# Causal attention: VectorE's split of a half's maxima placed directly behind the last of them

## The reference

```python
h = _layernorm(x, ln_w, ln_b)                        # then a causal depthwise convolution of 3 taps along T
q, k, v = jnp.split(h @ attn_w, 3, axis=-1)          # 16 heads of 8
q = q * cos + _rotate_half(q) * sin                  # k likewise
scores = jnp.einsum('bqhd,bkhd->bhqk', q, k) / jnp.sqrt(jnp.float32(D))
scores = jnp.where(causal, scores, jnp.float32(-1e+30))
p = jax.nn.softmax(scores, axis=-1)
y = jnp.einsum('bhqk,bkhd->bqhd', p, v).reshape(B, T, C)
x = x + y @ proj_w
```

## Time and profile before

| | us |
|---|---|
| median of 3 runs | 1636.36 (1632.52 to 1644.97) |
| profiled execution: its own time, its span | 1630.4, 1628.7 |
| causal attention in it | about 234 (236 to 470) |

### The profile page before, as it was taken

The page is one execution under the profiler, slowest core; times in us unless marked ns, Lnnn a source line. Parts: engine busy times, 40 slices in busy tenths (PEclk is TensorE's granted clock), DMA queues, the critical chain, the costliest instruction groups (busy, mean ns, idle before and its releaser), DMA issues. The chain is left out here.

```text
span 1628.7 us, 23696 instructions
## 1 busy us (share of the span) xinstructions
PE 1406.0 (86%) x9145; PEld 715.1 (44%) x9145; DVE 987.6 (61%) x1770; ACT 687.7 (42%) x1204; POOL 628.2 (39%) x626
## 2 busy tenths in 40 slices
PE   7868786988989999899868999899999877889984
PEld 3345443433334444444334444454445433355542
DVE  4898939777742211468566773745556344588866
ACT  2444432766742000257534774244434432355522
POOL 2487734354223221333124312533421312356762
PEclk8889997989999999879987998999999978999996
DMA  5000010000020000100001002000000010000000
GB/s 111 0 1 0 1 48 1 1 1 1 1 82 1 1 0 0 53 1 1 11 0 54 2 2 47 1 2 1 2 1 2 2 31 1 7 1 2 2 1 28
DMA packets 17382, 20.65 MB, mean 13 GB/s; under 512 B 7835, under 2 KB 13195, under 8 KB 16760
## 3 DMA queue, kind: packets, MB, share of 16 engines
q1 hardware_dynamic: 15440, 17.33, 3.6%
q10 hardware_dynamic: 1832, 1.80, 0.5%
HBM read 17.94 MB, written 1.05 MB: 12 GB/s over the span
## 5 line engine op out<-in xcount | busy, mean ns | idle before, releaser
L1852 DVE CUSTOM_DVE_ANT_0 P<-P,L2f_mask 128x128 f32<-128x128 f32 (+3 forms) x256 | 118.5, 521 | 99.9 <-PE P L1744 99.9
L1029 DVE TENSOR_REDUCE L0f_nm<-P 128x2 f32<-128x768 f32 (+3 forms) x88 | 97.5, 1120 | 38.1 <-PE P L926 37.9
L2028 PE MATMUL P<-L0m_hm,L0m_w 128*128 128x512 f32 x256 | 112.2, 597 | 0.0
L1822 ACT ACTIVATE L2f_prob<-P 128x1024 f32<-128x1024 f32 x80 | 80.6, 1025 | 73.1 <-PE P L1756 73.1
L1663 POOL TENSOR_SCALAR_AFFINE_SELECT L2f_prob<-L2f_prob 128x512 f32<-128x512 f32 x64 | 39.9, 638 | 161.4 <-ACT L2f_prob L1822 161.4
L983 ACT ACTIVATE L0f_prob<-P 128x512 f32<-128x512 f32 x160 | 86.9, 610 | 33.8 <-PE P L937 32.5
L1744 PE MATMUL P<-L2f_ks,L2f_qs 48*128 48x512 f32 (+3 forms) x512 | 90.9, 467 | 0.3 <-DVE L2f_nm L1852 0.3
L1756 PE MATMUL P<-L2f_qs,L2f_ks 49*128 49x256 f32 (+3 forms) x512 | 84.5, 444 | 3.1 <-DVE L2f_nm L1852 2.3
L2431 POOL TENSOR_TENSOR L3x_exm<-L3x_exm,L3x_rec 128x2048 f32<-128x2048 f32 x16 | 72.4, 4530 | 24.1 <-DVE L3x_rec L2617 24.1
L1306 PE MATMUL P<-ident,L0x_pv 128*128 128x128 f32 x384 | 53.7, 305 | 27.1 <-POOL L0x_pv L1207 27.1
L880 POOL TENSOR_SCALAR_AFFINE_SELECT L0f_prob<-L0f_prob 128x512 f32<-128x512 f32 x64 | 39.9, 638 | 95.2 <-ACT L0f_prob L983 88.3
(11 more groups left out here) (578 smaller groups left out, 3329.5 us busy)
## 6 DMA issues: line engine op xcount, KB each, us to landing
L0m_w<-in_L0m_w SPq DMA_DIRECT2D x1, 2048.0 KB, 8.0
L0f_va<-in_L0f_va SPq DMA_DIRECT2D x3, 512.0 KB, 5.3
L0x_prod<-in_x SPq DMA_DIRECT2D x2, 512.0 KB, 5.9
L0x_segi<-in_segb SPq DMA_DIRECT2D x1, 1024.0 KB, 18.2
L0m_w<-in_L0m_w SPq DMA_DIRECT2D x1, 1024.0 KB, 10.0
out<-out_o SPq DMA_DIRECT2D x4, 256.0 KB, 2.4
L1x_va<-in_va SPq DMA_DIRECT2D x3, 256.0 KB, 3.1
L1x_vr<-in_vr SPq DMA_DIRECT2D x3, 256.0 KB, 4.1
```

What stands on the lines that cost most here:

```text
L1029: nc.vector.tensor_reduce(S.nm[:, qt, first:first + 2 * many].rearrange("p (i e) -> p e i", e=2), P[:, bank:bank + 2, 0:many * width].rear ...
L1822: nc.scalar.activation(S.prob_of(b, g)[:, at:at + 2, :], P[:, bank:bank + 2, :], ACT.Exp).then_inc(*S.act_done.up())
L1852: m = nc.vector.tensor_tensor_reduce(out=at, in0=at, in1=mask[:, T - width:T], scale=1.0, scalar=-3.0e38, op0=ALU.add, op1=ALU.max, accum_ ...
L2028: m = mm(P[:, slot(b, i) + part, :], w1[:, e, part * 512 + i * 128:part * 512 + i * 128 + 128], hm[b % 2][:, e, :], start=e == 0, stop=e = ...
```

## The change

Two edits in causal_order, none to the instructions themselves.

```diff
-STEP_causal_order = """sa0 R0 w0 w1 R1 la A0 B0 t0 k0 ... R8 p0 A5 mb x0 R9 B1 sa1 mc p1 sb1 B5 mt B7 x1 R10 conv C1 out C3 sc1 max res""".split()
+STEP_causal_order = """sa0 R0 R1 la w0 w1 A0 B0 t0 k0 ... R8 p0 A5 mb x0 R9 B1 sa1 mc p1 R10 sb1 B5 max mt B7 x1 conv C1 out C3 sc1 res""".split()
...
-    lead = [(k, 0, n) for n in (2, 3) for k in ("t1", "tk")] + [(k, 1, n) for n in range(QT) for k in "px"] + [("conv", 2, 0)]
-    order += spread_between(lead, rounds(0)) + [("max", 0, 0)]
+    lead = [(k, 0, n) for n in (2, 3) for k in ("t1", "tk")] + [(k, 1, n) for n in range(QT) for k in "px"]
+    order += spread_between(lead, rounds(0)) + [("max", 0, 0), ("conv", 2, 0)]
```

More of the change, by code:

```diff
@@ L793, in split_pair @@
         ops.tensor_copy(k[:, :, :, 1], k[:, :, :, 4]).then_inc(*self.qk_ready.up())
-STEP_causal_order = """sa0 R0 w0 w1 R1 la A0 B0 t0 k0 R2 B2 A1 lb A2 R5 A4 C0 k1 R4 A6 lc lt rec sb0 sc0 B6 R3 B4 A3 R7 A7 ma C2 B3 R6 t1 turn R8 p0 A5 mb x0 R9 B1 sa1 mc p1 sb1 B5 mt B7 x1 R10 conv C1 out C3 sc1 max res""".split()
+STEP_causal_order = """sa0 R0 R1 la w0 w1 A0 B0 t0 k0 R2 B2 A1 lb A2 R5 A4 C0 k1 R4 A6 lc lt rec sb0 sc0 B6 R3 B4 A3 R7 A7 ma C2 B3 R6 t1 turn R8 p0 A5 mb x0 R9 B1 sa1 mc p1 R10 sb1 B5 max mt B7 x1 conv C1 out C3 sc1 res""".split()
 def causal_order(STEP=STEP_causal_order):
```

## The result

The changed kernel takes 1668.05 us (1665.09 to 1670.35), 1.0184 of the kernel before, with a 95% interval of 1.0141 to 1.0227; timed again on another chip (f_both below) it is 1.0200, 1.0157 to 1.0244. It is slower by about 31 us. The forecast was 13 us more, and its range ended at 1659: the sign was right, the size was not.

What follows compares the result with a forecast made beforehand. It took PE, busy for 86% of the span, as the bound. Terms -1.2 + 4.4 - 1.2 + 5.6 + 0.4 + 1.2 + 4.2 = +13.4 us gave 1649 us from a median of 1636.4, range 1636 to 1659.

Steps and rivals of the forecast that it cites:

- The split no longer ends last: At the ends of halves, w0's wait for the split, 20.8 us in all, would be gone or under 1 us.
- p + 3.75: Half 0 before: split's end counted from p, when p1 is done and PE takes up B5; forecast p + 3.4.
- rival 4: The split is hardly earlier where R10 follows p1, 0.4 us; counted within the forecast, with no chance of its own.
- C1 waits for x1, four times 4.3: Halves 0 to 3: x1 behind R10 and the split starts C1 4.0 us later, PE idle for 4.3.
- Rival 3: x1 does not stop PE at C1, so shifts and drops there are gone: -9 us, 1627; chance 0.13.
- The pair decides behind halves 1 and 3, and the shift goes through behind 0 and 2: POOL's pair sets t0 behind halves 1 (-1.2) and 3 (+0.4); w1's shift passes through behind 0 (+4.4) and 2 (+5.6).
- A0's exponential then follows w0 about 0.4 closer: Halves 4 to 6, with la ahead of w0: A0 follows w0 about 0.4 us closer, offsetting part of the delay.
- at most +0.9 each, nothing at least: Halves 4 to 6, which have no p1: delay from la behind tv, ahead of w0; +1.2 us taken for the three.
- Drops at the ends of all four halves ... 2 x 2.1 = +4.2: PE's clock falls behind the C1 waits of halves 0 to 3; costs 2.1 us each behind 0 and 2 only.
- Rival 2: The low clock stays 6.5 us or more behind each C1 stall: +20.6 us, 1657; chance 0.17.
- Rival 1: The clock is not dropped where it costs, or comes back at once: +9 us, 1645; chance 0.20.
- -1.2, between 0 and -2.3: The lead: convolution behind the split lets split and w0 go earlier, a gain of 1.2 us, at most 2.3.

Runs made afterwards that it cites:

- f_both: The changed kernel itself, timed again on another chip: 1.0200 of the kernel before.
- e6_x1_first: The changed kernel with x1 alone put back ahead of R10 and the split: 1653.67 us, 1.0098 of the kernel before.
- f_stall: The changed kernel with la put back behind w1, so x1 stays behind R10 and the split: 1.0093 of the kernel before.
- f_neither: The kernel before with only the convolutions behind the split and R1 ahead of w0: 0.9995 of the kernel before.
- the cells: Four kernels, x1 ahead of or behind the split and la behind or ahead, R1 ahead and convolutions behind: 0.9995 to 1.0200 side by side on one chip.
- e7_r1_only: The kernel before with the convolutions behind the split and R1, without la, ahead of w0 and w1: 1629.49 us, 0.9965.
- f_la: The kernel before with the convolutions behind the split and R1 and la ahead of w0, x1 in its old place: 1.0041.
- e2: The kernel before with the convolutions behind the split and R1 and la ahead of w0 and w1: 1649.45 us, 1.0120.
- e1: The kernel before with only the convolutions moved behind the split: 1632.86 us, 0.9989.
- e4_busy: The changed kernel with 16 matmuls of no use to the result in front of C1 in halves 0 to 3: 1665.62 us, 1.0183.
- e9_la_late: The kernel before with convolutions behind the split, R1 ahead of w0, and la ahead of w0 in halves 4 to 7 alone: 1636.13 us, 1.0019.
- e12: The changed kernel with la put back behind w1 in half 7 alone: 1653.40 us, 1.0115 of the kernel before.
- e8_lead_busy: The kernel before with convolutions behind the split and matmuls of no use to the result on PE in the lead: 1636.63 us, 0.9999.

## Why the prediction was right in sign and wrong in size

**The split no longer ends last: right.** Its wait fell from 20.8 us to 2.9. In half 0 that is not because the split came early: it ends 3.8 us behind R10's first product (301.69 to 305.47), where 3.4 was forecast and before it was p + 3.75, as rival 4 has it. It is w0 that comes later.

**C1 waits for x1, four times 4.3: right.** Four times 4.1, and e6_x1_first shows the cause: x1 ahead of R10 takes the wait away, and 14 us with it. The size of the wait was worked out from rows of before and met to 5%. Rival 3 (x1 does not stop PE) is refuted.

**The pair decides behind halves 1 and 3, and the shift goes through behind 0 and 2: right but for 1.2 us.** -1.2 forecast and measured behind half 1; +0.4 forecast and +1.6 measured behind half 3; +7.7 against +8.3 behind half 2, clock included. f_stall has this part alone: +14.9 in the trace of the stage, of which 4.1 stand in lead and half 0 of f_neither too.

**"A0's exponential then follows w0 about 0.4 closer" and "at most +0.9 each, nothing at least", for R1 and la ahead of w0: this step failed.** I priced la as a shift of w0 by its length and noted only in passing that it had covered ACT's copies. The forecast had about 3 us for la (1.0 each behind halves 0 and 2, and the +1.2; the working beside "+0.9" gives 1.0); the cells give it 1.0% of the kernel, some 16 us. The same edit for R1 costs nothing that can be told (e7_r1_only). What is seen in the traces is the cover lost: nine waits for ACT's copies, 5.0 us in all, against none or 0.3 with la behind. With x1 ahead of the split they use up what the shorter wait for the split gives (5.0 us in f_la). The stage is longer by 5 or 6 us with la ahead, in about equal parts of idleness and of slower matmuls (f_la less f_neither 2.5 and 3.2, e2 less e1 2.6 each); with x1 behind the split it is longer by 11 or 12, of which 6 or 7 are idleness and 5 slower matmuls. In half 7 the low clock came with la ahead, and for the clock there the forecast had no term at all.

**"Drops at the ends of all four halves ... 2 x 2.1 = +4.2": right where it looked.** The drops behind the C1 waits came. At the end of half 0 the changed kernel is at +9.5 and +9.1, e4_busy, at a clock of 1.00, at +4.4; less the 2.0 to 2.7 of the lead, the drop cost 2 to 3 us for 2.1 forecast. Rival 1 (the clock is not dropped where it costs) is refuted by these 2 to 3 us as far as one trace of each kernel can do it; the prediction's remark that the second rival is the case of no loss should name the first. Rival 2 (the low clock stays) has part of its condition: in this trace the clock is at 0.50 for 7 us behind C1, past its 6.5, but back at 1.00 when t0 starts at 315.38. It does not have its places: behind halves 1 and 3 the pair still hides the low clock. What the term lacked is the drops away from the C1 waits, in half 7 and in the lead.

**The lead, "-1.2, between 0 and -2.3": not found.** Lead and end of half 0 without the C1 wait are +3.6 in e1 and +4.1 in f_neither, because the low clock of the lead reached to about 296 us there and only to 286 in before's trace. e9_la_late, with the same lead, has it as in before (33.3 and 21.1 us), and e2, e4 and e12 have such a lead too (33.3 to 33.4); but none of these four is shorter than before's 33.4 by as much as 0.1, so the gain itself did not come. The longer lead is chance, or odds that the convolution's move has shifted; one trace of before can't tell these apart.

**Sum.** Stage +13.4 forecast, +27.1 and +26.1 measured; the timings say 31. Of the 13 missing in the traces, 6 are the last three columns, nearly all half 7 (la and the clock), 5 lead and half 0 (the lead's clock, and 1 more for the drop), 2 the ends of halves 2 and 3. The right sign is no luck: the step that the forecast priced best, x1 behind the split, makes the kernel slower by itself, by 15 us (f_stall, 1.0093). What the forecast lacks is about the price of la.

**What stays open.** The timings give la 16 us with x1 ahead of the split and 19 with x1 behind it (1.0192 - 1.0075); in the traces of the stage it is 5 or 6 (f_la less f_neither, 8.0 - 2.3; e2 less e1, 5.6 - 0.4) and 11 or 12 (26.1 - 14.9 and 27.1 - 14.6). The mean granted clock over the timed executions is 0.9013 and 0.9047 in the cell with la alone against 0.9123 and 0.9102 in the one with neither, by the slope in the last section some 9 us. That is an estimate: the slope is taken within kernels, and between the changed kernel and e4_busy it does not hold (0.010 more clock, no time). So the rest may be low clock in executions that were not traced; where in them it fell, no run here shows. And why the clock falls in half 7 with la ahead stays open.

A version that beats the kernel before by more than can be told was not found: f_neither, the one closest to it, is 0.9995 (0.9965 to 1.0024) after 0.9965 the first time.

## What to carry to other kernels

Before moving a step ahead of the one it follows, ask what it was covering there: la cost nothing where it filled PE's wait for ACT's copies, and about 1% where it did not (0.5% to 1.6% by the pairs of cells), though the wait for the split became shorter. On an engine that works in order, a producer moved forward pushes back what stood ahead of it; find whose buffer is then freed late (here the bank of p1, 4.1 us four times). And a wait taken away is worth what ends next: in two halves of four that was POOL's pair.

## What the runs showed of the hardware

The spread of one kernel's timings is mostly TensorE's clock. Over 300 timed executions of these kernels, each compared with its own kernel's mean on its chip, time falls by 11.3 us for every 0.01 of mean granted clock; this takes up 78% of the variance and leaves 3.5 us of a standard deviation of 7.3. Between kernels the slope need not hold: e4_busy has more clock than the changed kernel and the same time. A schedule can therefore cost time in two ways that have to be read apart: by the gaps that it makes, and by how often the clock falls at them.

What makes it fall is not the longest wait alone. In half 7 of the kernel before one wait of 1.55 us and five later gaps of 0.23 to 0.41 left the clock at 1.00, while gaps of 0.57, 0.55 and 0.23 among short pieces of work were followed by the low level in f_la. Which of the gaps matters, no run here shows. With la ahead of w0 in half 7, all eight traces have the low clock there (30.4 to 35.0 us for the stretch); with la behind, two of ten have it (both 31.7; the others 26.8 to 28.0, f_stall's 28.0 with some 3 us of low clock). Those two, e7_r1_only and e8_lead_busy, have the order of half 7 unchanged. This agrees with what the Trainium skill (TensorE: Matmul & The Clock Gate, "What's actually happening") says of a monitor that runs freely and not in step with the kernel: the same gaps cost something in one execution and nothing in another. Once low, the clock can stay low through unbroken work: in e4_busy PE is busy for 16.0 of the 16 us from 338 to 354, at 0.50 throughout. And where work was put in to keep PE busy, the clock was higher at that place in both trials (1.00 for 0.76 in e4_busy, 0.95 for 0.63 in e8_lead_busy), and the total time lower in neither.
